# Two heads a turn with six placing transfers in place of three with nine, and new orders of work in the body and at both ends of an attention tower

## The reference, cut to what matters

```python
h = tok(x)                                    # (64, 37, 256)
q, k, v = h @ Wq, h @ Wk, h @ Wv              # 16 heads of 64
sim = q @ k.T * 64 ** -0.5
sim = sim + cope(q, sim, pos_emb)             # cumulative gates pick entries of a table q @ pos_emb
out = softmax(sim) @ v                        # heads side by side
h = layernorm(h + out @ Wout + b_out)
# then 8 experts, 2 for each token, and a shared one, and a second layernorm
shared = silu(h @ sg) * (h @ su) @ sd
h = layernorm(h + shared + routed(h))
```

## Time and profile before

| | |
|---|---|
| median of 3 runs | 741.5 us (740.51 to 741.54) |
| profiled execution | 741.82 us, its span 740.1 us |
| PE busy | 690.8 us (93%) |
| DVE busy | 489.3 us (66%) |
| ACT busy | 418.5 us (57%) |

### The profile page before, as it was taken

How to read it: one execution, slowest core, us unless ns; L and a number is a source line. 1 busy time by engine, 2 the same in 40 slices (tenths; PEclk the granted TensorE clock), 3 DMA queues, 4 the chain that set the end, 5 groups by cost and what they waited for, 6 DMA issues and landing times.

```text
span 740.1 us, 14154 instructions
## 1 busy us (share of the span) xinstructions
PE 690.8 (93%) x4720; PEld 590.9 (80%) x4721; DVE 489.3 (66%) x1027; ACT 418.5 (57%) x730; POOL 122.8 (17%) x156
## 2 busy tenths in 40 slices
PE   8996899999999999999999996969799999999996
PEld 5895696969879696969789693848687999999885
DVE  3374687878978787878879787558582222222667
ACT  1653667576676667566675654532215777775363
POOL 2100000000000000000000000000003777775130
PEclk9998999999999999999999999889899999999999
DMA  8720131515141241414131114048003555552811
GB/s 275 207 64 15 37 72 49 97 49 99 54 93 50 66 83 34 95 51 83 54 65 46 36 43 131 23 117 285 21 1 83 136 141 136 142 139 63 277 66 52
DMA packets 85110, 67.17 MB, mean 91 GB/s; under 512 B 51277, under 2 KB 76347, under 8 KB 85079
## 3 DMA queue, kind: packets, MB, share of 16 engines
q1 hardware_dynamic: 80506, 56.73, 29.6%
q0 software_dynamic: 4224, 9.71, 4.4%
q10 hardware_dynamic: 348, 0.34, 0.1%
HBM read 35.60 MB, written 15.75 MB: 69 GB/s over the span
## 4 chain that ended last, share of the span: by engine, by line
PE 79%; SPq 7%; DMA 5%; ACT 5%; issue 3%; DVE 1%; ACTq 0%; DVEq 0%; POOLq 0%
PE ps_S L920 13%; PE ps_S L1408 10%; PE ps_X L1062 8%; PE ps_X L1014 7%; PE ps_S L999 7%; PE ps_S L1138 6%; PE ps_S L1420 5%; PE ps_S L1053 5%; PE ps_S L911 5%; SPq L637 4%; PE ps_S L1341 4%; PE ps_X L920 2%; PE ps_S L929 2%; PE ps_S L1036 1%; SPq L706 1%
## 5 line engine op out<-in xcount | busy, mean ns | idle before, releaser
L1014 PE MATMUL ps_X<-wkv_sb,hT 128*120 128x512 f32 (+1 forms) x176 | 83.1, 604 | 6.3 <-ACT v_sb L1518 6.3
L1408 PEld LDWEIGHTS ps_S<-attnT,v_sb 128*128 128x128 f32 x704 | 84.7, 192 | 4.9 <-ACT attnT L1748 2.8
L1408 PE MATMUL ps_S<-attnT,v_sb 128*128 128x128 f32 x704 | 85.9, 275 | 1.4 <-ACT attnT L1748 1.4
L1901 DVE COPY_PREDICATED table<-bit,table 111x112 f32<-111x112 int16 (+6 forms) x110 | 74.8, 680 | 11.2
L814 POOL TENSOR_TENSOR rs<-ve,neg_half 111x2 f32<-111x2 f32 x11 | 12.2, 1112 | 414.2 <-DVE ve L1987 414.2
L2332 DVE COPY attnT<-ps_S 128x256 f32<-128x256 f32 x44 | 18.7, 424 | 81.1 <-PE ps_S L1420 80.9
L920 PE MATMUL ps_S<-hT,wq_sb 128*128 128x216 f32 (+1 forms) x320 | 62.5, 347 | 5.2 <-ACT kT L1468 5.2
L1014 PEld LDWEIGHTS ps_X<-wkv_sb,hT 128*120 128x120 f32 (+1 forms) x176 | 28.9, 179 | 43.5 <-issue 28.9
L920 PEld LDWEIGHTS ps_S<-hT,wq_sb 128*128 128x128 f32 x320 | 56.4, 188 | 8.3 <-issue 7.0
L1062 PE MATMUL ps_X<-oT,wout_sb 128*128 128x222 f32 x320 | 62.9, 353 | 0.0
L1062 PEld LDWEIGHTS ps_X<-oT,wout_sb 128*128 128x128 f32 x320 | 59.3, 190 | 1.5 <-issue 1.5
(11 more groups left out here) (321 smaller groups left out, 1332.4 us busy)
## 6 DMA issues: line engine op xcount, KB each, us to landing
down_sb<-in_x_dram SPq DMA_DIRECT2D x10, 648.0 KB
gu_sb<-y_d SPq DMA_DIRECT2D x8, 512.0 KB, 6.6
attnT<-attn SPq DMA_DIRECT2D x126, 28.9 KB
h_d<-hT SPq DMA_DIRECT2D x11, 240.0 KB, 2.5
kept<-h_d SPq DMA_DIRECT2D x11, 240.0 KB, 2.7
h_d<-h SPq DMA_DIRECT2D x10, 222.0 KB
attnT<-attn SPq DMA_DIRECT2D x63, 34.7 KB
wkv_sb<-in_L_attn_Wkv_dram SPq DMA_DIRECT2D x2, 1024.0 KB, 12.4
```

The lines of the kernel that those rows point to most:

```text
L1014: mm = nc.tensor.matmul(X[:keyed, 1 - s], hT[:, k].rearrange("p b t -> p (b t)")[:, at:at + keyed], wkv_sb[:, k, INNER + 512 * s:INNER + 5 ...
L1408: mm = nc.tensor.matmul(S[:, i, j * FF + f * P:j * FF + f * P + P], held[:, i, k, j, f * P:f * P + P], xgT[:, i, k], start=(k == 0), stop= ...
L1901: A.did(V.copy_predicated(near[:, :, :, 0:SL - d], by_side(bit[:, n], r)[:, :, :, 0:SL - d], near[:, :, :, d:SL]))
```

## The change

1. **Two heads a turn.** `turn_weights` transposes two heads at a time (80 partitions): eight transposes in place of six, four to a bank. ACT's two copies have 444 columns in place of 333. The placing transfers are 2 x 3 = 6 a group in place of 9, with eight heads each.
2. **Two queues at the ends.** For groups 0, 19 and 20, SP issues three of the six transfers and ACT issues the other three, right after its copies in `weights`.
3. **Pair 1.** `outputs(0, 0)` moves from the head of the pair behind the scores and values; ACT's `gates(1, 0)` stands ahead of it. The first scores no longer wait for `ot_sb`.
4. **The body.** On ACT, `values(p, 0, 1)` moves ahead of `weights(2p - 1)`, and `gates(p, 0)` behind it. PE's wait for the last keys moves from ahead of `queries` to ahead of the `outputs` inside it.
5. **Pair 10 and behind it.** The turns 0 to 3 of the records fill the wait for group 19, with banks of their own; ACT's `distance(20)` moves ahead of `outputs(19, 1)`. Routing and parts of the shared expert move ahead of `outputs(20, 0)`; `distance(21)` comes after the first copy of the logits.
6. **SP's queue.** `store_halves(9)` moves between the two halves of the gate and up weights, and the down weights behind the last stores of rows.

The diff, cut to its core:

```diff
-        BLOCKS = -(-HEADS // TPG)
+        BLOCKS = HEADS // 2
+        PER_BANK = BLOCKS // 2
-        PLACES = TPG * TPG
+        PLACES = 2 * TPG
+        def to_diagonal(j, b):
+            return (own_T[PAD * b:PAD * b + PAD, b, j * BLOCKS:j * BLOCKS + BLOCKS],
+                    turned_attn[PAD * j:PAD * j + PAD, b])
+        def in_two_queues(g):
+            return isinstance(g, int) and (g == 0 or g >= G - 3)
+        ROUTES = (0, FULL - 1, 2, 4)
         def turned_in(c):
-            return X[:, 0] if c >= FULL else (S[:, 4], X[:, 0])[c % 2]
+            if c < 4:
+                return S[:, (4, 5, 2, 3)[c]]
+            return X[:, 0] if c == 5 or c >= FULL else S[:, 4]
...
 sync, place_attn:
-                for j in range(TPG):
-                    n, at = in_block[j], from_slot[j]
+                for j in range(2 - in_two_queues(g)):
                     for b in range(TPG):
-                        sp.dma_start(own_T[..., at:at + n], turned_attn[..., :n]).then_inc(placed[a], 16)
+                        sp.dma_start(*to_diagonal(j, b)).then_inc(placed[a], 16)
 sync, expert weights: in the loop over t
+                if t == 0:
+                    store_halves(G2 - 2)
-            (down weights, then store_halves(G2 - 2), here)
...
+            (down weights here, behind the last stores of halves)
 tensor, queries:
                     if s == 3 and not next_first(p):
+                        pe.wait_ge(k_sb, p * 4 + 4)
                         outputs(p * 2 - 2, 0)
 tensor, score:
-                        if f > 0:
+                        if f > 0 and not (next_first(p) and a == 0):
                             pe.wait_ge(ot_sb, p * 4 + f // 3 - 4 + 2 * a)
 tensor, pair:
                 if next_first(p):
-                    outputs(0, 0)
                     pe.wait_ge(xt_sb, p * 3 + 6)
                     score(p, 0)
                     values(p, 0, 1)
+                    pe.wait_ge(sim_sb, p * 4 + 2)
+                    pe.wait_ge(table_sb, p * 2 + 1)
+                    outputs(0, 0)
...
                     turn_weights(p * 2 - 1, True)
-                    turn(0)
+                    for c in range(2):
+                        turn(c)
                 values(p, 1, 1)
...
-                    pe.wait_ge(h1t_sb, 1)
+                    for c in range(2, 4):
+                        turn(c)
+                    pe.wait_ge(h1t_sb, 4)
                 outputs(p * 2 - 1, 1)
...
-                if ahead:
-                    pe.wait_ge(k_sb, p * 4 + 8)
-                else:
-                    pe.wait_ge(h1t_sb, FULL)
+                if not ahead:
                     pe.wait_ge(at_sb, 4 * (G - 1))
-                    for j in range(2):
-                        shared_part(0, 0, j)
+                    shared_part(0, 0, 0)
+                    for c in ROUTES[1:]:
+                        route(c)
+                    shared_part(0, 0, 1)
                     shared_part(0, 1, 0)
-                    outputs(p * 2, 0)
-                    pe.wait_ge(ot_sb, 2 * G - 2)
-                    for c in range(2, FULL, 2):
-                        route(c)
-                    shared_part(0, 1, 1)
                     pe.wait_ge(across_sb, FULL + 1)
                     by_half(0, EARLY)
+                    outputs(p * 2, 0)
+                    shared_part(0, 1, 1)
+                    pe.wait_ge(ot_sb, 2 * G - 2)
 scalar, weights(g, a): behind the two copies
+                if in_two_queues(g):
+                    act.wait_ge(attnT_zeroed, 1) if g == 0 else act.wait_ge(o_done, g * 2)
+                    act.wait_ge(at_sb, g * 4 + 4)
+                    for b in range(TPG):
+                        act.dma_start(*to_diagonal(1, b)).then_inc(placed[a], 16)
 scalar, pair:
                 score(p, 0)
+                if next_first(p):
+                    gates(p, 0)
+                    outputs(0, 0)
                 values(p, 0, 0)
                 if not ahead:
                     softmax_exp(p * 2 - 1)
-                else:
-                    weights(p * 2 - 1)
-                gates(p, 0)
                 values(p, 0, 1)
+                if ahead:
+                    weights(p * 2 - 1, 1)
                 if not next_first(p):
+                    gates(p, 0)
                     split(p - 2)
...
-                    weights(p * 2 - 1)
-                    turn(0)
+                    weights(p * 2 - 1, 1)
+                    for c in range(2):
+                        turn(c)
+                    distance(p * 2)
+                    for c in range(2, 4):
+                        turn(c)
                 outputs(p * 2 - 1, 1)
                 for s in range(2):
                     values(p, 1, s)
-                if not ahead:
-                    distance(p * 2)
                 score(p, 1)
...
-                    weights(p * 2)
-                    distance(p * 2 + 1)
-                    outputs(p * 2, 0)
+                    weights(p * 2, 0)
 scalar, behind the pairs:
-            for at, c in enumerate((0, 2, 4, FULL - 1)):
+            for at, c in enumerate(ROUTES):
                 logits_out(c, at)
+                if at == 0:
+                    distance(G - 1)
+            outputs(G - 2, 0)
             softmax_exp(G - 1)
```

More of the change, by code:

```diff
@@ L149, in vit_tower @@
         own_attn = attn_flat[:, :HEADS * PAD].rearrange("p (h j) -> p h j", h=HEADS)
-        BLOCKS = -(-HEADS // TPG)
-        in_block = [len(range(j, HEADS, TPG)) for j in range(TPG)]
-        from_slot = [sum(in_block[:j]) for j in range(TPG)]
+        BLOCKS = HEADS // 2
+        PER_BANK = BLOCKS // 2
         turned_attn = (attn_flat[:, HEADS * PAD:HEADS * PAD + BLOCKS * TPG * TOK]
@@ L707, in _ @@
                                  ).then_inc(w_exp, 16)
-            for t in range(KE):
-                sp.dma_start(down_sb[:, :, t, :], down_w[:, P * t:P * t + P, :].rearrange("e p n -> p e n")
-                             ).then_inc(w_exp, 16)
-            store_halves(G2 - 2)
+                if t == 0:
+                    store_halves(G2 - 2)
             sp.wait_ge(h1_ready, 2 * G2 + 2)
@@ L719, in _ @@
                 sp.dma_start(hh_d[row:row + r, :], h1_halves[a][:r]).then_inc(hh_stored[a], 16)
+            for t in range(KE):
+                sp.dma_start(down_sb[:, :, t, :], down_w[:, P * t:P * t + P, :].rearrange("e p n -> p e n")
+                             ).then_inc(w_exp, 16)
             for t in range(NT):
@@ L1088, in turn @@
                     pe.wait_ge(table_sb, G - 1)
[L1089 to L1091 removed]
+                elif c == 4:
                     pe.wait_ge(sim_sb, 2 * G)
                     pe.wait_ge(table_sb, G)
[L1094 removed]
+                elif c == 5:
+                    pe.wait_ge(v_ready, 2 * G)
+                elif c == FULL - 1:
                     pe.wait_ge(h1t_sb, c - 1)
@@ L1227, in pair @@
                 else:
-                    turn(1)
                     pe.wait_ge(ot_sb, p * 4)
                     residual_half(p - 1, X[:, 1], 0)
-                    turn(2)
+                    turn(4)
                     residual_half(p - 1, X[:, 1], 1).then_inc(res_done, 1)
-                    for c in range(3, 5):
-                        turn(c)
+                    turn(5)
+                    turn(6)
                     pe.wait_ge(res_ready, p * KE)
                     route(0)
-                    for c in range(5, FULL):
-                        turn(c)
                 if not ahead:
@@ L1627, in first_pair @@
                     queries(1, s)
-                weights(0)
+                weights(0, 0)
                 distance(1)
                 patches(2)
-                outputs(0, 0)
             def pair(p, ahead, ahead2):
@@ L1677, in pair @@
                 else:
-                    for c in range(1, 3):
+                    turn(4)
+                    softmax_exp(p * 2)
+                    for c in range(5, FULL):
                         turn(c)
-                    softmax_exp(p * 2)
-                    for c in range(3, FULL):
-                        turn(c)
-                    weights(p * 2)
-                    distance(p * 2 + 1)
-                    outputs(p * 2, 0)
+                    weights(p * 2, 0)
             act.dma_start(pe_nat[:TOK, :], pos_embed[0]).then_inc(w_small, 16)
```

29 lines of the change are left out of this document (14 added, 15 removed).

## The result

The changed kernel takes 717.9 us (median of 4 runs, 716.7 to 721.4) where the kernel before takes 741.5 on the same chip: a ratio of 0.968, with a 95% interval of 0.963 to 0.973. The forecast was 717.0. Its profiled execution took 716.74 us with a span of 715.0; PE is busy for 683.1 us of it (96%).

The account below looks back on a forecast made before the run. PE, busy 93%, was taken to bound the kernel, with DVE's ring less than 0.2 us a pair shorter and leading after the change. Terms: 741.8 - 5.6 - 12.0 - 7.2 = 717.0 us; range 710 to 727.

Parts of the forecast that it names:

- First term: Start and body: DVE 7.0 us ahead at pair 1's scan, 5.6 left at pair 9; -5.6 us.
- DVE's ring: Body: loop of scores, DVE's table, ACT's copies and gates, DVE's scan; 41.15 us, growing to 41.5 and leading.
- PE's sum: Body: two waits removed, 1.28 us a pair, four transposes added, 0.4; PE alone would gain 0.9 a pair.
- Rival 1: Body: DVE's ring does not bind and PE's own sum holds; 5.1 us better, 712 us; chance 0.12.
- The placing in the body: Body: six transfers save 2.25 us of issue, PE comes only 0.7 us earlier; costed at nothing.
- Second term: Last pair: no DVE wait for distance(20), group 21's transposes at 485.7 instead of 497.76; -12.0 us.
- Third term: Behind the last pair: earlier store removes PE's 4.02 us wait and the half clock after it; -7.2 us.
- Rival 2: Placing at the ends: two queues issue no faster than one; 5 us worse, 722 us; chance 0.13.
- the rule of the skill: Placing issues: descriptor block locked by one sequencer at a time, so three and three cost like six; 722 us.
- Rival 3: Behind the last pair: store still lands late behind 2 MB of loads, third term lost; 724 us; chance 0.1.
- Rival 4: Body: gates behind turn_weights make the kernel slower, needing 3.1 us a pair more; 744 us; chance 0.03.

Follow-up runs that it names:

- e3: The changed kernel with SP's old order behind the last pair, six weight loads and then store_halves(9): 726.4 us, 0.980 of before.
- e8: The changed kernel with outputs(20, 0) ahead of the routes, and on ACT its copies ahead of the logits' copies: 741.0 us against 763.8 before, 0.970.
- e2: The changed kernel with the body's order of before on ACT and PE, two heads and six transfers kept: 722.8 us, 0.975 of before.
- e1: The changed kernel with ACT's gates(p, 0) right behind the first value copy in the body: 708.6 us, 0.956 of before.
- e6: The changed kernel with three heads a turn and nine placing transfers a group again: 741.0 us against 763.8 before, 0.972.
- e10: The changed kernel with ACT's distance(20) behind the copies of outputs(19, 1) and of the values again: 718.1 us, 0.968 of before.
- e11: The changed kernel with all placing transfers issued by SP, at groups 0, 19 and 20 too: 716.4 us, 0.967 of before.
- e9: The kernel before with only SP's store_halves(9) moved behind two weight loads and the down loads behind the last stores: 732.9 us, 0.988 of before.
- e12: Second run of the changed kernel with early gates in the body and group 0's six transfers all by SP: 705.6 us, 0.953 of before.
- e5: First run of the changed kernel with early gates in the body and group 0's six transfers all by SP: 729.3 us against 763.8 before, 0.956.

## Why the prediction came out right, step by step

**First term, -5.6: measured -4.7.** The scan of pair 1 was put at 75.6 and came at 75.83. DVE's ring was put at 41.5 and measured 41.31: 0.37 was added for ACT's order, and 0.27 came. The term is 0.9 us off, and it is that near by two misses that run against each other. I moved DVE 7 us forward and asked nothing of what PE would be late with: DVE then stood 1.69 us for the embedding, behind `outputs(0, 0)` and `turn_weights`, and of the 6.75 us 4.49 were left at pair 2, a loss of 2.3 that the forecast doesn't have. The body, to which I gave 1.4 us of loss for DVE's longer ring, then gained 0.24. By e3 and e8 the start is worth only 3 us in the worse case of the clock. So the mechanism is right and the nearness of the number partly luck.

**PE's sum.** The added transposes were right (0.4 a pair; e2 shows 0.42). PE without waits was put at 41.32 - 0.9 = 40.4, and e1 has it at 40.0; what the other 0.4 are was not taken apart. Rival 1 is out: the ring of DVE binds, as e1 shows directly. The nearness of the two rings, 0.2 us, was the reading on which the body stood; e1 and e2 are its two sides.

**The placing in the body, costed at nothing.** That holds, but the reason given, that without fewer transfers PE's gain would have turned into a wait, was only half of it. It did turn into a wait (e6: 0.9 us a pair), and the pair was none the longer, since DVE led.

**Second term, -12.0: measured -12.7.** In the times of before (the trace's plus 4.73) the steps lie where they were put: `outputs(19, 1)` at 458.6 (458.8), group 21's logits done at 483.3 (483.6), `outputs(20, 0)` done at 482.3 (483.0), the transposes at 485.0 (485.7). The chain went by PE's residual: with DVE's wait for `distance(20)` put back, which I told first and at length, the time is the same (e10). The kernel before says it too, where DVE, behind the 6.88 us and its logits, still stood for the residual:

```profile
475.26 0.80 DVE L1971 SCALAR_TENSOR_TENSOR resT<-ps_X,posT,kept 128x222 f32<-128x222 f32 x2 [2.77 <-PE ps_X L1062]
```

By DVE's rows the 17.45 us at the transposes are the body's 4.73, 6.04 more at the scan (467.04 for 477.81), -0.17 to the logits, and 6.85 from the logits to the transposes (2.24 us for 9.09). For those 6.85 I had named two causes in one breath, ACT in the copies of `outputs(20, 0)` and PE in the placing. The runs say that either remedy is enough by itself. From group 21's scan to its transposes the kernel before takes 19.95 us; the changed kernel takes 13.27; e8, with the outputs back in their old place and six transfers in two queues, 13.22, and PE waits 1.20 us there where it stood 5.13 before; e6, with the new place and nine transfers in two queues, 13.12 (480.59 - 467.47); e11, with the new place and six in one queue, 13.30. So of the two causes in the forecast either alone, once gone, gives the whole gain. The old place with nine transfers in one queue and only the earlier turns was not run, so what the turns bring is open.

**Third term, -7.2: measured -7.6 in the trace,** and 8.5 either way round in e3 and e9. By e9's trace it is 7.0 behind the transposes. The chain of late store, `split(10)`, logits and half clock is shown. The loads that went behind it cost nothing: from the first tile to the end it is 175.4 us after and 175.5 before.

**Rival 2, and the rule of the skill.** ACT's and SP's issues ran side by side, 2.27 and 2.29 us for three each, 0.76 apiece, as long as SP alone needs. The Trainium skill, "Perfetto Trace Analysis", section "DMA Instruction — HWDGE (DVE, Sync)", has the block that makes descriptors locked by one sequencer at a time; these issue rows show no such turn-taking, though a lock held for less than half of an issue's 0.76 us would not show in them. At group 19 the landing came hardly sooner than with one queue, 5.87 against 6.01 us. At group 20 in e8 it came 474.62 - 470.57 = 4.05 us behind the first issue, sooner than SP alone could have issued six (4.51). One queue would have landed them there after 5.8 us by estimate (4.51, and 487.64 - 479.59 - 6.77 = 1.28 behind the last issue, by the kernel before at the same place). So turn-taking is not what held group 19. What stands there and not at group 20 are the 256 KB loads of `h_d`: the DMA engines are 0.94 busy from 446 to 448 us and idle from 469 to 470. That these loads are the cause was not tested. The kernel didn't take 722 for this reason, and because the landing at group 19 is nearly off the path: e11, without the second queue, is no slower.

**Rival 3** is out by the trace (no wait of ACT at 497.80). **Rival 4** needed 3.1 us more a pair; ACT's gates behind `turn_weights` cost 1.3 against where they could stand, as e1 shows, and nothing against before.

## What to carry to other kernels

When two rings of work have nearly the same length, an edit that shortens one brings at most the difference; look at which order of the shared engine (here ACT's gates against its copies) shortens the other as well, and the same edit may then bring 20 us, as the six transfers did only with early gates. A long wait in the profile is a candidate and not a gain: ask what its engine waits for next, since DVE's 6.88 us for `distance(20)` were worth nothing and a store's place in one queue 8.5 us. Before a trace's difference is put down to an edit, look whether it was there ahead of the edit: e8's 1.7 us were, and half of e12's 3.2 us came of the clock. Let the engine that is not on the path issue DMAs: ACT's three cost 2.4 us at the start, and the second queue landed group 19's 0.1 us sooner and group 20's, by estimate, 1.8 us, where nobody waited.

## What was not expected of the hardware

The same gap of PE is followed by either clock. A wait of 2.46 us in pair 1 was followed by outputs of 1.74 us in e11 and of 2.90 in e12:

```profile
71.93 1.74 PE L1065 MATMUL ps_S<-attnT,v_sb 120*64 120x111 f32 x32 [2.46 <-ACT simS L1498]
```

```profile
71.75 2.90 PE L1065 MATMUL ps_S<-attnT,v_sb 120*64 120x111 f32 x32 [2.46 <-ACT simS L1498]
```

So a gap of this size costs its length and sometimes 1 to 3 us more.

One kernel differs by 3% between two groups of runs, and in one stretch alone. The kernel of e5 and e12 reaches its tiles at 527.99 us in the one and 528.25 in the other, with body pairs equal to 0.01 us; its spans are 725.9 and 703.7. The expert tiles, whose rows are gathered, make the difference. Both groups carry the same chip number, so whether two chips differ here, or one at two times, is not shown. Stretch 600 to 640 us (PE busy first, granted clock, DMA share and GB/s last), of e5, then of e12:

```profile
600.00:640.00 40.00, 34.51 (x244) 30.59 (x243) 10.31 (x26) 25.03 (x39) 24.95 (x25) 1.00 0.44 114
```

```profile
600.00:640.00 40.00, 40.00 (x304) 38.23 (x304) 11.45 (x30) 29.73 (x46) 29.23 (x29) 1.00 0.51 127
```

The clock is full in both, and e5's PE stands where e12's does not. Which transfer comes late was not taken apart.
